# Slots of norms, roped low parts, scaled heads and a bias in the second stage of a two-stage transformer block

## The reference

```
x = x + attn_a(layernorm(x))    # 16 heads of 64; exact GELU on the heads, output product, + its own input
x = x + ffn(layernorm(x))       # relu(x @ Wq1.T + b1) @ Wq2.T + b2, Wq1 and Wq2 rounded to -1, 0, 1
x = x + attn_b(layernorm(x))    # 16 heads of 16; biases, rotary q and k, output product with bias
x = x + ffn(layernorm(x))       # the same FFN (256 -> 1024 -> 256) with the same weights again
```

## Time and profile before

| | |
|---|---|
| median of 3 runs | 4077.31 us |
| the profiled execution | 4078.41 us |
| its span | 4076.6 us |
| PE busy | 3760.2 us, 92% |
| DVE busy | 2718.1 us, 67% |
| ACT busy | 2350.2 us, 58% |
| POOL busy | 1930.6 us, 47% |
| granted TensorE clock | 0.981 of full speed on average |
| first scores of the second stage, last scores | 2437.4 us, 3993.4 us |

### The profile page before, as it was taken

How to read it: one execution, slowest core, us unless ns; L and a number is a source line. 1 busy time by engine, 2 the same in 40 slices (tenths; PEclk the granted TensorE clock), 3 DMA queues, 4 the chain that set the end, 5 groups by cost and what they waited for, 6 DMA issues and landing times.

```text
span 4076.6 us, 64388 instructions
## 1 busy us (share of the span) xinstructions
PE 3760.2 (92%) x23170; PEld 2647.2 (65%) x23170; DVE 2718.1 (67%) x4275; ACT 2350.2 (58%) x4529; POOL 1930.6 (47%) x1219
## 2 busy tenths in 40 slices
PE   7999999999999999999999878999999999999987
PEld 5777777777777777777777654555555555555534
DVE  5665666666566666656666657777777777777762
ACT  4655655556555565555656535666666666666654
POOL 3454545445455455544544543444444444444412
PEclk9999999999999999999999978999999999999988
DMA  4443444434344344343443523232333332222220
GB/s 129 94 101 91 92 93 101 92 91 104 92 90 104 91 91 102 91 99 87 101 101 81 128 39 54 51 54 54 54 57 55 54 58 53 53 53 53 48 43 16
DMA packets 152363, 315.51 MB, mean 77 GB/s; under 512 B 23088, under 2 KB 76720, under 8 KB 152048
## 3 DMA queue, kind: packets, MB, share of 16 engines
q1 hardware_dynamic: 152048, 311.39, 35.6%
HBM read 33.43 MB, written 25.17 MB: 14 GB/s over the span
## 4 chain that ended last, share of the span: by engine, by line
PE 54%; DVE 21%; ACT 14%; issue 7%; POOL 3%; SPq 1%; DMA 0%; DVEq 0%; POOLq 0%; ACTq 0%
PE ps_o L622 10%; DVE neg_max L947 7%; ACT e_a L775 6%; PE ps_t L216 5%; PE ps_o L699 5%; DVE max_b L1088 4%; ACT raw_a L799 3%; PE ps_t L725 3%; PE ps_s L672 3%; PE ps_t L658 3%; PE ps_m L734 3%; PE ps_t L223 3%; PE ps_t L606 3%; PE ps_t L734 3%; POOL h_lo L529 2%
## 5 line engine op out<-in xcount | busy, mean ns | idle before, releaser
L495 POOL TENSOR_TENSOR e_a<-e_a,recip 128x1024 f32<-128x1024 f32 x512 | 970.4, 1895 | 1049.8 <-DVE recip L954 1049.8
L775 ACT ACTIVATE e_a<-ps_s,neg_max 128x512 f32<-128x512 f32 x1024 | 694.9, 684 | 245.0 <-DVE neg_max L947 234.1
L1088 DVE TENSOR_REDUCE max_b<-ps_s 128x2 f32<-128x1024 f32 x512 | 623.2, 1218 | 227.5 <-PE ps_s L672 225.1
L815 ACT ACTIVATE et<-ps_s 128x1024 f32<-128x1024 f32 x512 | 523.8, 1023 | 393.9 <-PE ps_s L686 393.8
L947 DVE TENSOR_REDUCE neg_max<-ps_s 128x2 f32<-128x1024 f32 x512 | 621.3, 1213 | 19.1 <-PE ps_s L594 19.1
L622 PE MATMUL ps_o<-et_a,v_a 128*64 128x256 f32 x4096 | 470.3, 382 | 0.0
L606 PE MATMUL ps_t<-ident,e_a 128*128 128x128 f32 x2736 | 394.7, 275 | 42.3 <-DVE et_a L961 36.1
L593 PE MATMUL ps_s<-stack_a 128*128 128x512 f32 x1024 | 412.7, 403 | 9.3 <-ACT e_a L775 7.7
L529 POOL TENSOR_TENSOR h_lo<-h,h_hi 128x512 fp32r<-128x512 f32 x256 | 327.2, 1296 | 168.8 <-ACT h_hi L859 168.8
L594 PE MATMUL ps_s<-stack_a 128*128 128x512 f32 x1024 | 401.9, 392 | 0.0
L606 PEld LDWEIGHTS ps_t<-ident,e_a 128*128 128x128 f32 x2736 | 321.2, 141 | 111.2 <-DVE et_a L961 52.1
(11 more groups left out here) (198 smaller groups left out, 7939.6 us busy)
## 6 DMA issues: line engine op xcount, KB each, us to landing
stack_a<-raw_a SPq DMA_DIRECT2D x256, 384.0 KB, 4.7
stack_a<-raw_a SPq DMA_DIRECT2D x256, 256.0 KB, 4.3
stack_a<-raw_a SPq DMA_DIRECT2D x256, 128.0 KB, 3.5
q_stack<-roped_q SPq DMA_DIRECT2D x256, 64.0 KB
k_stack<-roped_k SPq DMA_DIRECT2D x256, 64.0 KB
x_a<-X SPq DMA_DIRECT2D x16, 512.0 KB, 3.7
X<-x_a SPq DMA_DIRECT2D x16, 512.0 KB, 2.9
x_ahead<-X SPq DMA_DIRECT2D x16, 512.0 KB, 3.8
```

The lines of the kernel that those rows point to most:

```text
L495: nc.gpsimd.tensor_tensor(e_a[:, u % 4, :, :], e_a[:, u % 4, :, :], factor, ALU.mult).then_inc(e_normed, 1)
L775: ins = nc.scalar.activation(e_a[:, u % 4, j, :], ps_s[:, 2 * (u % 2) + j, :], ACT.Exp, bias=neg_max[:, u % 4, j:j + 1], accum_out=sums[:, ...
L815: nc.scalar.activation(et[:, v % 5, :, :], ps_s[:, 2:4, :], ACT.Exp)\
L1088: nc.vector.reduce_max(max_b[:, u // 4 % 2, :, u % 4], ps_s[:, score_bank(u):score_bank(u) + 2, :], AX.X, negate=True).then_inc(max_done, 1)
```

## The change

Only slots of the second stage's tables change; no instruction is added, taken away or given another shape. In steps modulo 64, with the slot in brackets:

| item | before | after |
|---|---|---|
| norm of ffn0: statistics, statistics, aggregate | 24, 26, 29 (12, 13, 14) | 20, 22, 23 (10, 11, 11) |
| norm of ffn0: normalise, normalise | 33, 34 (16, 17) | 25, 30 (12, 15) |
| norm of attn: second normalise | 5 (2) | 6 (3) |
| norm of ffn1: first normalise | 50 (25) | 49 (24) |
| bias of ffn1, on POOL | 55 (27) | 60 (30) |
| low parts of roped q | 31, 32 (15, 16) | 33, 34 (16, 17) |
| low parts of roped k | 36, 37 (18, 18) | 36, 38 (18, 19) |
| scaled heads, quads 0 and 1 | 44, 60 (22, 30) | 46, 62 (23, 31) |
| load of ffn0's input | 15 (7) | 13 (6) |

```diff
-        NORM = {"ffn0": (-104, -102, -99, -95, -94), "attn": (-67, -64, -63, -60, -59), "ffn1": (103, 108, 109, 114, 115)}
-        BIAS = {"ffn0": -88, "attn": -57, "ffn1": 119}
-        ROTATE, HIGHS, LOWS = (-39, -37, -35, -34, -32, -30), (-34, -33, -29, -28), (-33, -32, -28, -27)
+        NORM = {"ffn0": (-108, -106, -105, -103, -98), "attn": (-67, -64, -63, -60, -58), "ffn1": (103, 108, 109, 113, 115)}
+        BIAS = {"ffn0": -88, "attn": -57, "ffn1": 124}
+        ROTATE, HIGHS, LOWS = (-39, -37, -35, -34, -32, -30), (-34, -33, -29, -28), (-31, -30, -28, -26)
         STACK = (-18, -16, -11, -9, 5, 7, 21, 23)
+        INVERT, SCALE_HEADS = (42, 58, 74, 90), (46, 62, 76, 92)
@@
-                            if r == -113:
+                            if r == -115:
                                 load_ahead(s)
@@
-                            if r >= 42 and (r - 42) % 16 == 0 and (r - 42) // 16 < QUADS:
-                                invert_sums(QUADS * s + (r - 42) // 16)
-                            if r >= 44 and (r - 44) % 16 == 0 and (r - 44) // 16 < QUADS:
-                                scale_heads(QUADS * s + (r - 44) // 16)
+                            if r in INVERT:
+                                invert_sums(QUADS * s + INVERT.index(r))
+                            if r in SCALE_HEADS:
+                                scale_heads(QUADS * s + SCALE_HEADS.index(r))
```

## The result

The changed kernel takes 4005.15 us (median of 4 runs, 4003.56 to 4007.47) against 4076.4 us for the kernel before in the same comparison (4075.45 to 4078.02). The ratio is 0.9825, with a 95% interval of 0.9808 to 0.9842. The profiled execution took 4003.56 us, its span is 4001.8. The forecast was 4016: right in direction, and the gain of 71 us was forecast as 61.

A forecast was written before the change was run, and what follows sets the result against it. PE, 94% busy, was taken to bound the second stage. A steady window gains 1.5 + 0.3 + 0.3 + 2.3 = 4.4 us, x 13 = 57.2, plus 4 in the end windows, 61 in all: 4016 us, range 3995 to 4046.

The forecast's parts named there:

- slot 19 against slot 27: Same PE work, 4.10 against 2.69 us, so 0.96 us of recorded wait for DVE's maximum stood for 1.41.
- Bias: Slot 28: with ffn1's bias behind the eighth low part, PE's 1.4 us wait for POOL goes; 1.5 us, bounds 1.2 and 1.7.
- 5.8 us in which PE stands idle: Steady windows of 100.3 us: PE's idle time was taken as the most a window can lose.
- Slots 15 to 20: Moving ffn0's norm earlier and low parts later shortens DVE's work ahead of the maxima; 2.3 us, bounds 0.7 and 3.3.
- Slot 23: Moving scaled heads and ffn1's first normalise removes the 0.35 us wait for the maximum; 0.3 us, bounds -0.3 and 0.5.
- Attn's half: Second half of attn's norm goes behind slot 3's maximum, removing a 0.49 us wait; 0.3 us, bounds 0 and 0.5.
- Start: Before the first window, POOL waits for sample 1's load, up to 4 us lost, 2 to 4 back; 0, bounds +3, -2.
- Load: ffn0's input is ready at 2939.8, its first statistics come at 2944.9: 5 us of slack, so no cost.
- The moving waits: Rival: DVE's blocked time only changes its slot; 2.2 us a window, 30 in all, 4047 us; chance 0.20.
- All of it is free: Rival: every part gains its full bound, 6.0 us a window, 83 in all, 3994 us; chance 0.12.
- The slower rival: DVE stands at ffn0's statistics if the load lands over 5 us later than its median; 4103 us; chance 0.03.
- the bounded middle: Nothing is felt, as PE would be held by ACT alone all through; 4077 us; chance 0.03.

The follow-up runs named there:

- the halved bias: The changed kernel with ffn1's bias as two additions of 128x512, the first back at step 55, the second at step 60: 4019.64 us (ratio 0.9848).

## Why the prediction came out as it did

*What bounds the kernel.* Right: PE sets the time, and the gain came from its waits for DVE and POOL. The estimate of what a recorded wait is worth (slot 19 against slot 27) held to the hundredth: 1.41 us.

*Bias, 1.5 forecast, 1.65 measured, and 0.55 beside it that the sum lacked.* The mechanism is as written. POOL after, in slot 28:

```profile
2973.96 1.30 POOL L530 TENSOR_TENSOR h_lo<-h,h_hi 128x512 fp32r<-128x512 f32 x1 [0.65 <-ACT h_hi L860]
2975.22 2.38 POOL L524 TENSOR_TENSOR x_before<-x_before,b_rows 128x1024 f32<-128x1024 f32 x1
```

The low part begins when ACT is done, and the bias has nothing behind it. What failed is the step "5.8 us in which PE stands idle" as the most that a window can lose: in four of the eleven windows PE's busy time held 1.5 us that the slow clock had made. The row had it, a granted clock of 0.99 and not 1.00; I did not ask in which slot. This is 0.55 of the 1.2 us by which the window's sum fell short. For the same reason the windows before do not repeat each other within some tenths, as was said of them: seven took 99.66 to 99.84 us, four 101.17 to 101.37.

*Slots 15 to 20, 2.3 forecast, 2.94 measured.* The direction of each of the parts was right, the time by which POOL blocks DVE was put too high. POOL's last rotations of q and DVE beside them, slots 14 to 16:

```profile
2933.68 2.99 POOL L543 TENSOR_TENSOR q_rot<-q_rot 128x512 f32<-128x512 f32 x2
```

```profile
2934.64 0.88 DVE L1126 TENSOR_TENSOR token_rows<-token_rows,recip_b 128x512 f32<-128x512 f32 x1
...
2936.19 1.19 DVE L1089 TENSOR_REDUCE max_b<-ps_s 128x2 f32<-128x1024 f32 x1
2937.30 2.06 DVE L1067 TENSOR_SCALAR xn<-x_ahead,mean_var,rstd 128x256 f32<-128x256 f32 x2
```

The normalisations took 2.06 us as forecast from the earlier trace rows, but in a slot that can hold them. The heads of slot 14 took 0.88 us, not the 1.78 of the earlier trace rows: DVE came in near the border of POOL's two instructions (the first ended at 2934.97), and POOL's pair took 2.99 us, where two rotations free of DVE took 2.53 in the kernel before. The value of 2.3 was set below the 3.0 us of worth on account of such blocking in the slots 14 and 15, and this was mis-sized: the slots 15 to 19 gained 3.05 us. The prediction had said that they would come out at 3.0 if port time were shared in proportion. They did, and yet the rows show blocking (2.06 us for two normalisations), so this sum was no test between the two. The last part of the step, that slot 20 gives back 0.3 us, came out as 0.11.

*Slot 23, 0.3 forecast, 0.41 measured, for a wrong reason.* I expected the multiplication to be blocked up to 1.78 us by the hidden low part. POOL and DVE after, in slot 23:

```profile
2959.97 1.02 POOL L518 TENSOR_TENSOR rstd<-rstd,minus_half 128x4 f32<-128x4 f32 x1 [12.48 <-DVE rstd L1060]
2960.96 1.80 POOL L530 TENSOR_TENSOR h_lo<-h,h_hi 128x512 fp32r<-128x512 f32 x1
```

```profile
2960.93 0.68 DVE L1126 TENSOR_TENSOR token_rows<-token_rows,recip_b 128x512 f32<-128x512 f32 x1
...
2962.47 1.23 DVE L1089 TENSOR_REDUCE max_b<-ps_s 128x2 f32<-128x1024 f32 x1
2963.62 2.43 DVE L1067 TENSOR_SCALAR xn<-x_before,mean_var,rstd 128x256 f32<-128x256 f32 x2
```

DVE began at 2960.93, 0.03 us ahead of POOL, and took 0.68 us (0.66 in slot 22 before, where POOL rests); POOL took 1.80 us in place of 1.28. It is the same in all 11 windows. The Trainium skill ("SBUF — State Buffer", section "Who interferes with whom") calls the shared port an exclusive lock, held for a whole instruction. Both rows agree with it. The forecast had read it in one direction only.

*Attn's half, 0.3 forecast, 0.02 measured.* "I take 0.3" failed on ACT's slack of 0.27 us: it was read as time that PE could give back, but it is a wait for something that PE does before the removed wait. The lower bound, 0, was the value, and the wait for ACT in slot 5 rose to 0.82, not 0.5.

*Start, 0 forecast, 2.3 lost.* The wait of POOL was as said (2398.35 against 2395.05, in place of 2399.3), but what was to come back did not: sample 1's four normalisations took 5.20 us beside POOL's rotations, and 1.37 us before, when POOL rested. DVE's rows, before and after:

```profile
2406.50 1.37 DVE L1066 TENSOR_SCALAR xn<-x_ahead,mean_var,rstd 128x256 f32<-128x256 f32 x4
...
2398.41 5.20 DVE L1067 TENSOR_SCALAR xn<-x_ahead,mean_var,rstd 128x256 f32<-128x256 f32 x4 [1.13 <-POOL rstd L518]
```

*Load.* No cost, as forecast: nothing in PE's waits of the steady windows goes back to it, and the slots 10 and 11 are as they were.

*The rivals.* The moving waits fail on the slots 15 to 19, which kept 0.18 of 2.57 us, but for the slots 3 to 5 they had it right: that wait moved. "All of it is free" had 6.0 us a window, and 5.58 were measured, 0.56 of them by a clock that it did not have. Its 3994 is as far from 4005 as the forecast of 4016, so the total does not choose between them; the slots do. The slower rival and the bounded middle have nothing in the trace.

*What the sum owes to luck.* The misses of a window were +0.15, +0.55, +0.64 and +0.11 against -0.28 us, and the start took 2.3 us against them. So attn's half and the start hid a part of what the clock and the slots 15 to 20 gave beyond the forecast.

## What to carry to other kernels

Ask of each removed wait what the next late engine itself waits for: if that is something ahead of the wait, its slack is nothing, and the wait only moves (slot 3 to slot 5). Where equal slots with equal work differ in length while PE is busy in both, read the granted clock slot by slot: a wait that ends just before can cost more than its length. And test edits of neighbouring slots together, for on an engine that works in order one can be worth little until the other is made (1.90 and 0.29 us, but 2.94 together).

## What the hardware showed that was not expected

A single idle time of 1.41 us of PE, in windows where it is otherwise busy 94%, was followed by a slot with a granted clock of 0.68 in 13 of 44 windows, each such slot 1.5 us longer; in the ten profiles without the long wait there was none in 110 windows, 11 of them with the halved bias and its waits of at most 0.4 us at that place. And where DVE began 0.03 us ahead of POOL, it had its free duration, 0.68 us, and POOL paid, 1.80 for 1.28, in 11 of 11 windows; elsewhere DVE paid (2.06 us for two normalisations that take 0.8 free by the earlier trace rows). So a small shift of a slot can change which engine is slow.
